# Query products of the mix stage: high and low parts stacked in the contraction, one rounded matmul of 96 rows in place of a full float32 one

## The reference, cut to what matters

```python
edge_index = jnp.stack([src, dst])
xn = _layernorm(x, axis=-1)                       # x: 1250 x 1024
x = x + gnn(xn, edges...) + mix(xn, gamma, w_q, w_kv, w_out)
x = x + ffn(_layernorm(x, axis=-1), ...)

def mix(x, gamma, w_q, w_kv, w_out):              # 8 heads of 16
    q, k, v = heads of rms_norm(x, gamma) @ (w_q, w_kv)
    q = taylor(q * 16 ** -0.5); k = taylor(k)     # taylor(x) = [1, x, (x_i x_j) / sqrt(2)]
    kv_state = einsum('bhnd,bhne->bhde', k, v)
    den = einsum('bhnd,bhd->bhn', q, sum of k over n)
    out = einsum('bhnd,bhde->bhne', q, kv_state) / maximum(den, EPS)
    return out @ w_out
```

## Time and profile before

| | before |
|---|---|
| time, median of 3 runs | 1711.09 us (1710.4 to 1714.0) |
| the profiled execution | 1710.35 us |
| its span, first to last instruction | 1708.5 us |
| TensorE busy | 93% of the span |
| VectorE, ScalarE, GpSimd busy | 52%, 23%, 46% |
| mean granted TensorE clock | 0.976 of full |

### The profile page before, as it was taken

One profiled execution on the slowest core, in us unless ns is written; L12 is line 12 of the kernel. 1 busy time (PEld: TensorE's weight loads), 2 busy tenths in 40 slices (PEclk: granted clock), 3 DMA queues, 4 the chain that ended last, 5 costly groups with the idle time before them and its releaser, 6 DMA issues.

```text
span 1708.5 us, 19085 instructions
## 1 busy us (share of the span) xinstructions
PE 1594.3 (93%) x7188; PEld 1276.0 (75%) x7188; DVE 892.7 (52%) x1324; ACT 393.9 (23%) x581; POOL 784.3 (46%) x672
## 2 busy tenths in 40 slices
PE   4999999999999999999999999999899959977988
PEld 4987777666667678888788787877777748866887
DVE  6534222334331420002887888785567737777885
ACT  3321111221122112222222222222211122232220
POOL 4426676656564135545545554654655641210110
PEclk8999999999999999999999999999999979988999
DMA  4422232322232222226778777867987864540001
GB/s 154 139 97 83 77 94 86 102 84 84 85 92 96 75 82 93 87 83 213 254 237 279 242 261 258 272 220 246 332 284 259 277 227 150 183 136 1 38 38 47
DMA packets 120458, 262.47 MB, mean 154 GB/s; under 512 B 23451, under 2 KB 37010, under 8 KB 120360
## 3 DMA queue, kind: packets, MB, share of 16 engines
q1 hardware_dynamic: 48568, 109.34, 18.9%
q0 software_dynamic: 33056, 83.02, 16.0%
q10 hardware_dynamic: 38736, 68.83, 10.8%
HBM read 193.33 MB, written 80.06 MB: 160 GB/s over the span
## 4 chain that ended last, share of the span: by engine, by line
PE 62%; DVE 19%; DMA 9%; issue 5%; ACT 3%; POOL 2%; ACTq 0%; SPq 0%; POOLq 0%; DVEq 0%
PE ps L1749 45%; DMA source_rows<-relation_rows,row_list 7%; PE ps L1988 5%; PE ps L1852 3%; DVE u_sum L1506 3%; PE ps L2020 2%; PE ps L1872 2%; DVE source_rows L1490 1%; PE ps L1832 1%; PE ps L2038 1%; ACT source_rows_hi L2163 1%; PE ps L1864 1%; DMA u_sum<-u_rows 1%; POOL WL L829 1%; DVE wq_rows L559 1%
## 5 line engine op out<-in xcount | busy, mean ns | idle before, releaser
L1749 PE MATMUL ps<-WH,XTH 128*128 128x512 f32 (+1 forms) x1680 | 670.9, 399 | 0.0
L1749 PE MATMUL ps<-WL,XTH 128*128 128x512 f32 (+1 forms) x1680 | 653.1, 389 | 0.0
L1749 PE MATMUL ps<-WH,XTL 128*128 128x512 f32 (+1 forms) x1680 | 653.0, 389 | 0.0
L1749 PEld LDWEIGHTS ps<-WH,XTH 128*128 128x128 f32 x1680 | 318.1, 189 | 81.9 <-issue 22.5
L829 POOL TENSOR_TENSOR WL<-RAW,WH 128x512 fp32r<-128x512 f32 (+1 forms) x184 | 239.3, 1304 | 304.4 <-ACT WH L2098 302.2
L1749 PEld LDWEIGHTS ps<-WH,XTL 128*128 128x128 f32 x1680 | 317.1, 189 | 64.5
L1749 PEld LDWEIGHTS ps<-WL,XTH 128*128 128x128 f32 x1680 | 317.5, 189 | 60.3 <-issue 2.4
L887 POOL DMA_INDIRECT source_rows<-relation_rows,row_list x180 | 222.2, 1234 | 264.6 <-PE ps L1872 134.5
L2120 ACT ACTIVATE EV<-ps 128x512 f32<-128x512 f32 x180 | 107.3, 596 | 610.9 <-PE ps L1749 541.1
L908 POOL DMA_INDIRECT edge_lists<-edge_words x160 | 197.0, 1231 | 46.3 <-issue 42.2
L1506 DVE SCALAR_TENSOR_TENSOR u_sum<-source_rows,weight_list,u_sum 128x1024 f32<-128x1024 f32 x120 | 168.4, 1404 | 74.6 <-DMA source_rows<-relation_rows,row_list 64.5
(11 more groups left out here) (301 smaller groups left out, 1515.9 us busy)
## 6 DMA issues: line engine op xcount, KB each, us to landing
relation_rows<-EV ACTq DMA_DIRECT2D x160, 256.0 KB, 2.1
RAW<-in_L_gnn_weight SPq DMA_DIRECT2D x128, 256.0 KB, 2.7
u_rows<-u_sum SPq DMA_DIRECT2D x20, 512.0 KB, 5.1
RAW<-in_L_gnn_w_gate SPq DMA_DIRECT2D x32, 256.0 KB, 4.6
mix_rows<-mix_rows_out ACTq DMA_DIRECT2D x10, 512.0 KB, 2.6
root_rows<-EV ACTq DMA_DIRECT2D x20, 256.0 KB, 4.3
u_sum<-u_rows SPq DMA_DIRECT2D x10, 512.0 KB, 7.3
bias_rows<-root_rows SPq DMA_DIRECT2D x10, 512.0 KB, 7.0
```

The source lines that it names most:

```text
L1749: mm = t_.matmul(ps[:, bank, 0:w], a[:, t, k, :], b[:, s, k, 0:w], start=(k == 0 and j == 0), stop=(k == KT - 1 and j == 2))
```

## The change

The key sums and the queries are each split into a rounded high part and the rest, the low part. For each group of two heads the three products of parts are one contraction over 96 rows: rows 0 to 31 are query high with key high, rows 32 to 63 query high with key low, rows 64 to 95 query low with key high. The moving operand has 290 columns in place of 289.

- Key side, once: after the copy of KVM (now written rounded) ScalarE writes four 32x580 blocks (KVS rows 0 to 31); VectorE's `key_parts` makes the low part from PSUM (two operations of 290 numbers) and writes eight 32x580 blocks (rows 32 to 95).
- Query side, for each tile: ScalarE's `query_high` writes two copies of the rounded, scaled queries (256 numbers a row); VectorE's `query_low` the rest (128 numbers). TensorE transposes four blocks of 96 columns in place of one of 128, now into bank 0; ScalarE copies 96x512 back. QT lies over KVM.
- `query_heads`: two rounded matmuls of 96 rows and 290 columns in place of two full float32 ones of 32 rows and 289. The wait for `mix_copied` moves from `query_t` to it.
- `query_high` for tile t+1 stands in ScalarE's second step of tile t, `query_low` for t+1 on VectorE ahead of group 2 (the third) of tile t.

```diff
-            ("key_value", [P, 2, FA * FA], F32), ("value_sums", [P, HEADS, FA], F32),
+            ("key_value", [P, 2, KVW], F32R), ("value_sums", [P, HEADS, FA], F32),
+            ("key_value_parts", [P, 3, 2, KVW], F32R))
+        KVS = [KVS_[:, 0], KVS_[:, 1], KVS_[:, 2], KV_LAST[:]]
+        QT = KVM[:].rearrange("p b e -> p (b e)")[:, 0:4 * P].rearrange("p (g n) -> p g n", g=4)
+            def key_parts():
+                dve.wait_ge(key_done, NT)
+                dve.wait_ge(kvm_ready, 3)
+                for b in range(2):
+                    part = v.scalar_tensor_tensor(KVL[:, b, :], ps[:, 2 + b, 0:KVW], parity[:, b:b + 1],
+                                                  KVM[:, b, :].bitcast(F32), ALU.mult, ALU.subtract)
+                part.then_inc(kv_parts, 1)
+                dve.wait_ge(kv_parts, 1)
+                for g in range(4):
+                    v.tensor_copy(KVS[g][32:64], KVL[pair]).then_inc(kv_parts, 1)
+                for g in range(4):
+                    v.tensor_copy(KVS[g][64:96], KVM[pair].bitcast(F32)).then_inc(kv_parts, 1)
+            def query_low(t):
+                dve.wait_ge(q_hi, t + 1)
+                v.scalar_tensor_tensor(QS[:, :, 2, :], QK[:, s, 0:HID].rearrange("p (g i) -> p g i", g=4),
+                                       DH ** -0.5, QS[:, :, 0, :], ALU.mult,
+                                       ALU.subtract).then_inc(q_lo, 1)
...
+            key_parts()
+            query_low(0)
             for t in range(NT):
                 for group in range(4):
+                    if group == 2 and t + 1 < NT:
+                        query_low(t + 1)
                     query_group(t, group)
                 attention(t)
...
             def query_t(t):
-                pe.wait_ge(qk_in[s], 16 * ((NT + t) // 2 + 1))
-                pe.wait_ge(kvm_ready, 3)
-                need(pe, mix_copied, t)
-                t_.transpose(ps[:, 2, 3 * P:4 * P], QK[:, s, 0:HID], ident[:]).then_inc(q_ps, 1)
+                pe.wait_ge(q_lo, t + 1)
+                need(pe, q_copied, t)
+                for g in range(4):
+                    mm = t_.transpose(ps[0:96, 0, P * g:P * (g + 1)],
+                                      QS[:, g].rearrange("p j i -> p (j i)"), ident[:])
+                mm.then_inc(q_ps, 1)

             def query_heads(t, group):
                 pe.wait_ge(q_copied, t + 1)
                 need(pe, g_used, 4 * t + group)
-                pair = slice(2 * DH * group, 2 * DH * (group + 1))
+                need(pe, mix_copied, t)
+                if t == 0:
+                    pe.wait_ge(kvm_ready, 3 + group + 1)
+                    pe.wait_ge(kv_parts, 1 + 4 + group + 1)
                 for b in range(2):
-                    mm = t_.matmul(ps[:, 2 + b, 0:FA * FA], QT[pair, :], KVM[pair, b, :], start=True,
-                                   stop=True)
+                    mm = t_.matmul(ps[:, 2 + b, 0:KVW], QT[0:96, group, :], KVS[group][0:96, b, :],
+                                   start=True, stop=True)
                 mm.then_inc(g_ps, 1)
...
             def key_sums():
+                act.wait_ge(kvm_ready, 3)
+                for g in range(4):
+                    a.activation(KVS[g][0:32], KVM[pair].bitcast(F32), ACT.Copy).then_inc(kvm_ready, 1)
+            def query_high(t):
+                act.wait_ge(qk_in[s], 16 * ((NT + t) // 2 + 1))
+                need(act, q_ps, t)
+                q = QK[:, s, 0:HID].rearrange("p (g i) -> p g i", g=4)
+                a.activation(QS[:, :, 0:2, :].bitcast(F32R), q.unsqueeze(2).broadcast_to([P, 4, 2, 2 * DH]), ACT.Copy,
+                             scale=DH ** -0.5).then_inc(q_hi, 1)
             def copy_queries(t):
-                a.activation(QT[:], ps[:, 2, 3 * P:4 * P], ACT.Copy, scale=DH ** -0.5).then_inc(q_copied, 1)
+                a.activation(QT[0:96], ps[0:96, 0, :].rearrange("p (g n) -> p g n", g=4),
+                             ACT.Copy).then_inc(q_copied, 1)
...
                     key_sums()
+                    query_high(0)
...
                     copy_queries(ti)
+                if 0 <= ti < NT - 1 and at == 1:
+                    query_high(ti + 1)
```

More of the change, by code:

```diff
@@ L56 @@
 FA = DH + 1
+KVW = FA * FA + 1
 I_FF = 352
@@ L250, in gps_layer @@
         XG, = stage_tensors(("source_rows", [P, 4, D], F32R))
-        QK, VT, KVM, V0, QT, AT, ATT, OHD, DENR = stage_tensors(
+        QK, VT, KVM, V0, _, AT, ATT, OHD, DENR, KVS_ = stage_tensors(
             ("qkv_tile", [P, 2, 3 * HID], F32), ("values1", [P, HEADS, FA], F32),
-            ("key_value", [P, 2, FA * FA], F32), ("value_sums", [P, HEADS, FA], F32),
+            ("key_value", [P, 2, KVW], F32R), ("value_sums", [P, HEADS, FA], F32),
             ("q_t", [P, P], F32), ("attn", [P, P], F32), ("attn_t", [P, P], F32),
-            ("heads_out", [P, HEADS, FA], F32), ("den", [P, 2, HEADS], F32))
+            ("heads_out", [P, HEADS, FA], F32), ("den", [P, 2, HEADS], F32),
+            ("key_value_parts", [P, 3, 2, KVW], F32R))
         TH = keep("TH", [P, 2, KT, P], F32R)
@@ L278, in gps_layer @@
         XTH = keep("XTH", [P, NT, KT, P], F32R)
+        KV_LAST, = stage_tensors(("key_value_last", [P, 2, KVW], F32R))
         ACC0 = keep("u_sum0", [P, D], F32)
@@ L352, in gps_layer @@
         dve_b = sem("dve_b")
+        kv_parts = sem("kv_parts")
+        q_hi = sem("q_hi")
+        q_lo = sem("q_lo")
         q_ps = sem("q_ps")
@@ L428, in gps_layer @@
         TMPQ = flat_b[:, 0:2 * DH * FA].rearrange("p (h j e) -> p h j e", h=2, e=FA)
+        KVL = flat_b[:, 2 * FA * FA:2 * FA * FA + 2 * KVW].rearrange("p (b e) -> p b e", b=2)
+        QS = flat_b[:, 4 * FA * FA + 2:4 * FA * FA + 2 + 12 * 2 * DH].rearrange(
+            "p (g j i) -> p g j i", g=4, j=3)
         REDQ = flat_b[:, 2 * DH * FA:2 * DH * FA + 2 * FA].rearrange("p (h e) -> p h e", h=2)
@@ L1443, in values_and_keys @@
                     key_features(v, s, half, f_ready[half])
+            def key_parts():
[7 more added lines that the diff above has]
+                for g in range(4):
+                    pair = slice(2 * DH * g, 2 * DH * (g + 1))
+                    v.tensor_copy(KVS[g][32:64], KVL[pair]).then_inc(kv_parts, 1)
+                for g in range(4):
+                    pair = slice(2 * DH * g, 2 * DH * (g + 1))
+                    v.tensor_copy(KVS[g][64:96], KVM[pair].bitcast(F32)).then_inc(kv_parts, 1)
+            def query_low(t):
+                s = t % 2
+                dve.wait_ge(q_hi, t + 1)
+                v.scalar_tensor_tensor(QS[:, :, 2, :], QK[:, s, 0:HID].rearrange("p (g i) -> p g i", g=4),
+                                       DH ** -0.5, QS[:, :, 0, :], ALU.mult,
+                                       ALU.subtract).then_inc(q_lo, 1)
             def query_group(t, group):
@@ L1840, in query_t @@
             def query_t(t):
-                s = t % 2
-                pe.wait_ge(qk_in[s], 16 * ((NT + t) // 2 + 1))
-                pe.wait_ge(kvm_ready, 3)
-                need(pe, mix_copied, t)
-                t_.transpose(ps[:, 2, 3 * P:4 * P], QK[:, s, 0:HID], ident[:]).then_inc(q_ps, 1)
+                pe.wait_ge(q_lo, t + 1)
[4 more added lines that the diff above has]
+                mm.then_inc(q_ps, 1)
             def query_heads(t, group):
@@ L2134, in key_sums @@
                 for p in range(2):
-                    a.activation(KVM[:, p, :], ps[:, 2 + p, 0:FA * FA], ACT.Copy,
+                    a.activation(KVM[:, p, :], ps[:, 2 + p, 0:KVW], ACT.Copy,
                                  scale=parity[:, p:p + 1]).then_inc(kvm_ready, 1)
@@ L2142, in copy_queries @@
                 need(act, g_ps, 4 * t)
-                a.activation(QT[:], ps[:, 2, 3 * P:4 * P], ACT.Copy, scale=DH ** -0.5).then_inc(q_copied, 1)
+                if t == 0:
+                    act.wait_ge(kvm_ready, 3 + 4)
+                    act.wait_ge(kv_parts, 1 + 8)
+                a.activation(QT[0:96], ps[0:96, 0, :].rearrange("p (g n) -> p g n", g=4),
+                             ACT.Copy).then_inc(q_copied, 1)
             def copy_attention(t):
```

## The result

The changed kernel takes 1685.45 us (median of 4 runs, 1680.5 to 1688.1), the kernel before 1711.42 (4 runs). The ratio is 0.984, 95% interval 0.982 to 0.986: 26 us faster. In a second session the same two kernels took 1686.2 and 1715.1 us, ratio 0.983, interval 0.980 to 0.986. The forecast was 1685.0. The profiled execution took 1685.22 us, its span is 1683.5.

What follows compares the result with a forecast made beforehand. VectorE's loop was taken to pace groups 2 to 4 on busy TensorE; 2.59 us a tile, 25.9 for ten, less 0.4 at the key side, gave 25.5 off 1710.35, stated as 1685.0 us, range 1680 to 1691 (1678 to 1699 with rivals).

Steps and rivals of the forecast that it cites:

- What bounds the stretch: Query products: TensorE is nearly always busy, but VectorE's 2.12 us a group already holds groups 2 to 4 a little.
- First group and transposes: Each tile: last weight matmul to VectorE's start falls from 1.67 to 0.77 us, gain 0.90; three more transposes cost 0.33.
- Groups 2 to 4: Later head groups of a tile: VectorE's loop falls from 3.58 to 2.89 us, gain 0.69 each, 2.07 for three.
- Attention: Attention's transpose in each tile: its load of 0.14 us is no longer partly covered, a loss of 0.05 us.
- The four terms: Each tile: first group 0.90, groups 2 to 4 2.07, transposes -0.33, attention -0.05, together 2.59 us.
- The start: Key side, once: extra copies and low parts before TensorE's first transposes cost 0.4 us, range 0 to 1.4.
- Does it arrive: Stretches behind the queries: stepped by TensorE, they move forward as a whole, so the 25.5 us gain reaches the end.
- rival B: Experiments' rival: gather stretch gives back part of the queries' gain, a sixth in the spread kernel's expectation; no chance given.
- Rival 1: Query tiles: VectorE's loop doesn't bind, TensorE gets all its time back, 4.7 us a tile, 1663 us; chance 4%.
- Rivals 3, 4 and 5: Query stretch: dearer head matmuls, 1691, 12%; late low part, 1717, 2%; falling clock, 1733 if a third at half, 2%.

Runs made afterwards that it cites:

- full float32: Changed kernel with the same 96 rows and 290 columns, but head products as full float32 again: 1721.24 us, ratio to before 1.003.
- the spread kernel: Changed kernel with a tile's small work placed elsewhere, head groups four blocks apart in place of three: 1672.58 us, ratio to before 0.975.

## Why the prediction was right, point by point

**What bounds the stretch.** Right, and shown: halving VectorE's work brings the groups to TensorE's pace, and spreading them does too.

**First group and transposes.** From the last weight matmul, 308.02, to VectorE, 308.83, it is 0.81 us; forecast 0.77. Two rounded matmuls in 0.28 us, as scaled from 352 columns. The four transposes start 0.11 us apart and cost 0.32 more a tile (forecast 0.33):

```profile
304.83 0.39 PE L1791 MATMUL ps<-WH,XTL 128*128 128x512 f32 x1
...
305.06 0.60 PE L1886 MATMUL ps<-ident,prefix 128*96 128x128 f32 x4
...
305.41 0.48 PE L1791 MATMUL ps<-WH,XTH 128*128 128x512 f32 x1
...
305.73 0.39 PE L1791 MATMUL ps<-WL,XTH 128*128 128x512 f32 x1
```

(305.73 less 304.83 less two spacings is 0.45. The one transpose before had cost 0.13, by the same reading of its neighbours.)

**Groups 2 to 4, the term that was mis-sized.** The loop is 2.81 us on average, not 2.89, so the three give 2.31 us and not 2.07. I had added the pieces at their largest. The two matmuls with their exposed load take 0.51 us, where 0.11, 0.136 and 0.30 make 0.55; the release takes 0.10 and not 0.11; and VectorE starts 0.03 behind the matmuls and not 0.11 in the one loop of three that has `query_low` ahead. Thirty loops make this 2.4 us.

**Attention.** Forecast a loss of 0.05; from VectorE's start to the second weight matmul behind the transpose it is 3.65 us, before 3.71: a gain of 0.06. One microsecond in ten tiles. The four terms, each read at one tile, add up to 2.91 us a tile; measured are 3.00. Averaged over all ten tiles of both traces they are 0.88, 2.35, 0.07 and -0.31, 2.99 together: the single tile of before that I read lies 0.01 to 0.03 under its kernel's average in the first three.

**The start.** I took 0.4 us for the key side. GpSimd, VectorE and TensorE after the change:

```profile
282.04 1.28 POOL L843 TENSOR_TENSOR WL<-RAW,WH 128x512 fp32r<-128x512 f32 x1 [4.93 <-ACT WH L2144]
282.05 1.42 DVE L1479 SCALAR_TENSOR_TENSOR prefix<-qkv_tile,prefix 128x128 f32<-128x128 f32 x1
...
283.52 0.64 PE L1886 MATMUL ps<-ident,prefix 128*96 128x128 f32 x4 [0.22 <-DVE prefix L1479]
```

and the one transpose before:

```profile
283.69 0.27 PE L1845 MATMUL ps<-ident,qkv_tile 128*128 128x128 f32 x1
```

The weight matmul ahead of the transposes starts at 282.92, so they were due 0.227 later, at 283.15 (the changed kernel came to the stretch 0.54 us ahead), and are 0.37 late. The number is right by accident. The eight copies take 0.45 us each, below the 0.51 I took, and would have been in time. The estimate by the Trainium skill, VectorE: DVE Perf Modes, section "The perf-mode tier table", was 0.46 for a copy of 580, and the trace agrees: the copies keep that rate with a rounded output. The late one is `query_low(0)`, 1.42 us and not 0.29, because GpSimd worked beside it; the prediction had named GpSimd only as one that waits.

**Does it arrive.** Forecast yes, and by the medians it does: between kernels of one session the time moves as the end of the mix does. Before to changed it is 28.9 us (end of the mix 30.2, or 29.3 with the second execution of before), full float32 to rounded 35.1 (32.6), changed to halved VectorE 15.1 (15.3), changed to spread 13.6 (14.5, by the first sum of gathered rows). Two or three microseconds either way may hide in each of these. The widest pairs decide: the spread kernel is 2.3 to 2.7% under before, 40 to 47 us, and its first sum starts 43.7 or 44.7 us earlier; with a sixth given back, as rival B had it, it would be 36 or 37. The kernel with VectorE's work halved is 40 to 49 us under before, and a sixth given back would leave it 37 or 38.

The single pair of traces had shown 5 of 30 us lost, and the first session's medians four. That was scatter of the late stretches. Over the executions seen, the sums took from 576 to 583 us whatever stood ahead of them, and the part from the first feed-forward matmul to the end 174.1 us (before), 175.9 (changed) and 176.3 (before again). What makes them scatter stays open. In the nine runs with full float32 the mean granted clock goes along with the time: the shortest, 1710.3 us, had 0.982, and the five over 1721 had 0.974 to 0.976. In the twelve of before the two go together less closely, and no run here shows which follows from the other.

So that the forecast of 1685.0 met 1685.45 to half a microsecond is luck, two errors against each other: the stretch gave four microseconds more than worked out, and the medians measured first kept 26.0 of its 29.5. The mechanism was right, and a gain of 29 us too would have come out within the stated 1680 to 1691. The second session's 28.9 us is nearer to what the change is worth. Rival 1 was far off (a tile of 21.5, not 19.7), and the spread kernel shows on what terms it comes true. Rivals 3, 4 and 5 did not come: no issue gap ahead of the first group, `query_low` in time for all tiles but the first, the clock of the stretch at 1.00.

## What to carry to other kernels

When one engine's step is made cheaper inside a ring of two engines, work out the other engine's share of the ring first: it is what is left. If it exceeds the filler between the steps, move the steps apart; here one block more between the groups was worth 13.6 us, on top of the 28.9 that the change had given. And judge what arrives at the end by medians of many runs, since two traces of one kernel differed by 5 us in stretches that the change never touched.

## What the runs showed of the hardware

GpSimd can make VectorE wait. A VectorE operation with two SBUF inputs of 128 numbers takes 0.29 us alone and 1.39 to 1.42 when GpSimd's 1.28 us operation with two SBUF inputs has started just ahead of it, a copy of 580 numbers 1.56 in place of 0.45; both end 0.15 to 0.3 us after GpSimd's. VectorE's reduction (L1495, 1.10 to 1.15 us) and its multiply with one input in PSUM (L1493, 0.72) take the same time with such an operation beside them and without. The Trainium skill, SBUF — State Buffer, section "SBUF: two separate sides", has one pair of ports that the two share and that one of them holds for a whole instruction while the other stands; the trace agrees where GpSimd starts first, and no run here shows the other order.

A stationary operand of 32 rows between operands of 128 has its own load and the next one unhidden: 0.30 us a tile here, at the first group and behind the fourth, since VectorE's loop covers it between them. With 96 rows neither load shows.
